# When VectorE turns the softmax denominators: small work moved between quarters of a unit, and the order of GpSimd's adds

## What is computed

```python
x = x + attention(layernorm(x), ctx, ctx)   # 32 query heads of 32 columns, 8 key/value heads,
                                            # softmax(q k^T / sqrt(32)) v
x = x + ffn(layernorm(x))                   # 8 small experts, the best one picked for each row
```

## Time and profile before

| | |
|---|---|
| median of three runs | 1024.35 us |
| the profiled execution | 1022.49 us |
| its span in the trace | 1020.7 us |
| granted TensorE clock, mean | 0.995 of full speed |

### The profile page before, as it was taken

The page is one execution under the profiler, slowest core; times in us unless marked ns, Lnnn a source line. Parts: engine busy times, 40 slices in busy tenths (PEclk is TensorE's granted clock), DMA queues, the critical chain, the costliest instruction groups (busy, mean ns, idle before and its releaser), DMA issues.

```text
span 1020.7 us, 24586 instructions
## 1 busy us (share of the span) xinstructions
PE 947.1 (93%) x9518; PEld 371.1 (36%) x9518; DVE 902.3 (88%) x1106; ACT 730.8 (72%) x1301; POOL 801.6 (79%) x454
## 2 busy tenths in 40 slices
PE   4789999999999999999999999999999999999996
PEld 3223333333333333333333323333222225777773
DVE  6979999999999999999999999998888886888976
ACT  5367788888888888888888877888777777554440
POOL 6259999999999999999999999999999998222110
PEclk9999999999999999999999999999999999999998
DMA  8674776767676767676867685756655744766423
GB/s 246 191 172 109 165 169 155 166 152 169 149 169 154 173 145 176 142 171 148 184 142 179 132 192 129 182 121 153 121 119 138 163 93 147 246 209 233 159 104 164
DMA packets 319875, 164.18 MB, mean 161 GB/s; under 512 B 182216, under 2 KB 307240, under 8 KB 319760
## 3 DMA queue, kind: packets, MB, share of 16 engines
q1 hardware_dynamic: 319456, 161.76, 64.3%
q0 software_dynamic: 304, 0.85, 0.4%
HBM read 107.58 MB, written 54.53 MB: 159 GB/s over the span
## 4 chain that ended last, share of the span: by engine, by line
PE 35%; DVE 31%; issue 25%; ACT 5%; POOL 3%; DMA 1%; SPq 0%; DVEq 0%; POOLq 0%; ACTq 0%
DVE row_max L927 14%; PE psum L590 8%; PE psum L604 6%; PE psum L617 5%; PE psum L735 5%; DVE den_t L939 4%; PE psum L552 4%; ACT probs L864 3%; PE psum L713 3%; DVE o_t L933 3%; DVE probs L1138 2%; PE psum L578 2%; DVE prod_mem L985 2%; PE psum L701 1%; ACT prod_mem L817 1%
## 5 line engine op out<-in xcount | busy, mean ns | idle before, releaser
L864 ACT ACTIVATE probs<-psum 128x512 f32<-128x512 f32 x1024 | 554.7, 596 | 131.0 <-PE psum L590 113.0
L927 DVE TENSOR_REDUCE row_max<-psum 128x4 f32<-128x2048 f32 x248 | 565.8, 2281 | 64.3 <-PE psum L552 64.0
L590 PE MATMUL psum<-q_stack,k_stack 97*32 97x512 f16 x4096 | 334.8, 386 | 9.9 <-issue 3.5
L365 POOL TENSOR_TENSOR sums<-probs 128x2048 f32<-128x2048 f32 x63 | 287.7, 4566 | 17.5 <-ACT probs L864 17.4
L353 POOL TENSOR_TENSOR sums<-probs 128x2048 f32<-128x2048 f32 x63 | 287.2, 4559 | 7.1 <-PE psum L627 5.5
L604 PE MATMUL psum<-probs,v_in 128*32 128x512 f32 x2048 | 268.8, 598 | 1.0
L590 PEld LDWEIGHTS psum<-q_stack,k_stack 97*32 97x32 f16 x4096 | 96.7, 95 | 258.8 <-ACT probs L864 149.2
L552 PE MATMUL psum<-high_mem 32*128 32x512 f16 x992 | 98.0, 384 | 23.7 <-DVE row_max L927 20.1
L325 POOL TENSOR_TENSOR o_t<-o_t,inv 128x512 f32<-128x512 f32 x64 | 67.2, 1049 | 40.7 <-DVE inv L945 38.8
L330 POOL TENSOR_TENSOR o_all<-o_all,o_t 128x512 f32<-128x512 f32 x64 | 81.6, 1274 | 9.2
L604 PEld LDWEIGHTS psum<-probs,v_in 128*32 128x32 f32 x2048 | 59.2, 110 | 60.9 <-issue 16.2
(11 more groups left out here) (119 smaller groups left out, 759.2 us busy)
## 6 DMA issues: line engine op xcount, KB each, us to landing
q_stack<-q_split SPq DMA_DIRECT2D x192, 128.0 KB, 3.4
xa<-in_x_dram SPq DMA_DIRECT2D x32, 512.0 KB, 4.7
o_all<-in_x_dram SPq DMA_DIRECT2D x256, 64.0 KB, 2.4
x_attended<-o_all SPq DMA_DIRECT2D x64, 256.0 KB, 4.1
out_dram<-probs SPq DMA_DIRECT2D x32, 512.0 KB, 2.9
q_split<-prod_mem SPq DMA_DIRECT2D x15, 1024.0 KB, 5.3
xa<-x_attended SPq DMA_DIRECT2D x16, 512.0 KB, 4.5
probs<-x_attended SPq DMA_DIRECT2D x16, 512.0 KB, 4.7
```

The costliest lines, as they stand in the source:

```text
L365: pool.tensor_tensor(sums[:, 2 * u % SUMS], probs[:, u % 2, 0], probs[:, u % 2, 1], ALU.add).then_inc(front_done, 1)
L590: last = pe.matmul(st_ps[row:row + D, bank_of["score", u, n], :], k_stack[:, u % SLOTS, t * P + row:t * P + row + D], q_stack[:, u % SLOTS ...
L864: act.activation(probs[:, s, keys, g, :], st_ps[:, bank_of["score", u, n], :], ACT.Exp, scale=EXP_SCALE).then_inc(exped, 1)
L927: dve.reduce_max(row_max[:, u % 2, t:G * ST:ST], s_ps[:], AX.X).then_inc(reduced, 1)
```

## The change

VectorE's list is changed in four places. The denominators of even units are turned in e1 instead of e0 (`DEN_AT`), behind that quarter's maxima, and their inverses are taken in e2 instead of e1. The inverses of odd units are taken in o3 instead of o1. The second half of a tile's moments moves from e1 to e2, and its variance from e2 to o1. In the planner, the denominator of an even unit is taken to keep its bank for 9 uses instead of 5. GpSimd adds the front pair of unit u ahead of the normalisation of unit u - 2 and of the inverse root, instead of behind them. No instruction is added or removed.

```diff
--- before.py
+++ after.py
@@ -195,7 +195,7 @@
 
             BEGIN = ((0, 4, 9, 13, NSC), (0, 4, 8, 12, NSC))
             MIDST = ((2, 6, 11, 15), (2, 6, 10, 14))
-            NORM_AT = 13
+            NORM_AT, DEN_AT = 13, 1
             DOWN_AT, FOLD_AT = ((-AHEAD, ST - 1), (1 - AHEAD, 0)), (1 - AHEAD, ST - 1)
 
             filled = [("part", n, i) for n in range(FIRST) for i in range(PIECES)]
@@ -211,7 +211,7 @@
                     filled += scores[half:]
                     if t == (ST - 1 if u % 2 == 1 else 2) and live(u - 1):
                         filled.append(("den", u - 1, 0))
-            KEPT = {"score": 2, "max": 2, "den": (5, 5), "part": 6}
+            KEPT = {"score": 2, "max": 2, "den": (9, 5), "part": 6}
             bank_of, bank_before, free_at, last_in = {}, {}, [0] * BANKS, [None] * BANKS
             for i, use in enumerate(filled):
                 bank = min(range(BANKS), key=lambda b: free_at[b])
@@ -355,15 +355,15 @@
                     if u == UNITS - 1:
                         for t in range(ST):
                             row_root(0, 0, t)
-                    if live(u - 2):
-                        normalise(u - 2)
-                    if u % 2 == 1 and whole(tile_of(u) + 1):
-                        inverse_root(tile_of(u) + 1)
                     if 0 <= u < UNITS - 1:
                         wait(pool, exped, NSC * u + NSC // 2)
                         wait(pool, den_done, u - 1)
                         pool.tensor_tensor(sums[:, 2 * u % SUMS], probs[:, u % 2, 0], probs[:, u % 2, 1],
                                            ALU.add).then_inc(front_done, 1)
+                    if live(u - 2):
+                        normalise(u - 2)
+                    if u % 2 == 1 and whole(tile_of(u) + 1):
+                        inverse_root(tile_of(u) + 1)
 
                 for n in range(ST + 2, TILES):
                     row_root(n // ST, n // ST % GROUPS, n % ST)
@@ -1032,19 +1032,19 @@
                             largest(*maxima_at(u, t))
                         if late and t < PIECES:
                             low_part(n, t)
-                        if t == 0 and live(u - 2) and u % 2 == 0:
-                            take_denominators(u - 2)
                         if u == UNITS and t == 0:
                             sum_last(1)
                         if t == 0 and live(u - 1):
                             take_rows(u - 1)
-                        if t == 1 and live(u - 2):
+                        if t == DEN_AT and live(u - 2) and u % 2 == 0:
+                            take_denominators(u - 2)
+                        if t == (DEN_AT + 1 if u % 2 == 0 else ST - 1) and live(u - 2):
                             invert(u - 2)
                         if early and t == 0 and u == 0:
                             first_moments(n + 1)
-                        if early and t == 1:
+                        if early and t == 2:
                             last_moments(n + 1)
-                        if early and t == 2:
+                        if late and live(u) and t == 1 and whole(n + 1):
                             variance(n + 1)
                             guard(n + 1)
                         if live(u) and u % 2 == 1 and t == ST - 1 and whole(tile_of(u + 1) + 1):
```

## The result

The changed kernel takes 1076.71 us in the median of four runs (1067.85 to 1077.35). The kernel before takes 1022.4 us, the median of the three runs above and a fourth of 1020.46 us. The ratio over all runs is 1.0513, with a 95% interval of 1.046 to 1.0566: slower by 5% (the medians alone give 1.053). The forecast was 1071 us, 1056 to 1081, slower with a chance of 0.88. The profiled execution is the 1067.85 us one, with a span of 1066.0 us; the other three took some 9 us more.

What follows compares the result with a forecast made beforehand. No engine was full; the handover between TensorE's score_rows and VectorE's maxima set the pair's length. Terms 24 x 1.6, 4 x 1.0, 2 x 0.66, 0.3 and 4.6 made 48.6 us; with 1022.5 that gave 1071 us, range 1056 to 1081.

Steps and rivals of the forecast that it cites:

- The bound and the maxima of e1: VectorE rules e0; with one transpose fewer there, the maxima of e1 start at 3.65 instead of 3.88, gaining 0.23 us a pair.
- The denominators: Turned behind the maxima of e1, they hold TensorE at tile 6 until 6.73 instead of 5.03; score_rows of e2 1.1 us late.
- What e2 adds: ScalarE's five late tiles delay the odd unit's denominators; score_rows of e3 comes at 11.3 instead of 9.69, 1.6 us late.
- The moves at no cost: Even and odd inverses, moments, variance and GpSimd's order fit into idle time or slack: cost 0.
- The tail: At u = 64 unit 62's transpose stands behind sum_last and take_rows, so project(0, 0) is late: 4.6 us, bounds 2 and 5.5.
- The sum: Over the whole kernel, the terms of the pairs and the end add 48.6 us to 1022.5, giving 1071 us.
- cheaper stall: Rival, chance 0.13: ScalarE catches up inside e2 and only 1.1 us a pair remain, so 1058 us.
- GpSimd ties in: Rival, chance 0.07: the 0.8 us slack at take_rows is gone, normalisation 0.5 late each pair, 15 us more: 1087.
- Faster: Rival, chance 0.07: TensorE reaches the tile later than 6.73, so den_taken costs no wait and the even spread pays: 1012 us.
- No change: Rival, chance 0.05: the bank is not as read and only the 0.23 us of e0 comes back: 1020 us.

Runs made afterwards that it cites:

- e0: Not a run: a quarter of the even unit in a pair of units; the kernel before turned the even denominators there.
- e3: Not a run: the quarter after e2 of the even unit in a pair; its score_rows was forecast at 11.3 instead of 9.69.
- The run with the wait at tile 4: The changed kernel with the planner's 5 uses of before, so the denominators' bank goes to tile 4 of e1: 1176.98 us, ratio 1.1501.

## Why the prediction was right

**The bound and the maxima of e1.** As forecast: the maxima of e1 start 3.64 us after `score_rows` of e0 (forecast 3.65), and e0 is TensorE's.

**The denominators.** The transpose starts at 5.85 (forecast 5.86), tile 6 at 6.61 (forecast 6.73), `score_rows` of e2 at 7.37 (forecast 7.39). TensorE goes on 0.05 us after the transpose's end, where I had taken 0.17 from the earlier trace rows.

**What e2 adds.** This term was too high by 0.2 us a pair. 0.12 us of it is the earlier tile 6. ScalarE starts its five tiles 0.45 us behind tile 6, and the odd unit's denominators come 3.0 us after that (430.81), where I had 3.1. They use the bank that ScalarE's small L796 frees behind the five tiles, at 430.71:

```profile
427.80 2.56 ACT L864 ACTIVATE probs<-psum 128x512 f32<-128x512 f32 x5 [1.85 <-PE psum L590]
430.44 0.27 ACT L796 ACTIVATE shift<-psum 16x128 f16<-16x128 f32 x1
```

`score_rows` of e3 comes at 11.07 instead of 11.3, which is 1.38 us late and not 1.6. Over 24 pairs I had 38.4 us and the profile shows 33.1. For tile 7 the pairs show 0.90 us (forecast 1.0), for tile 8 0.66 and 0.67 (forecast 0.66).

**The moves at no cost** are shown to be so by the run with the denominators put back. In detail the idle 0.57 us ahead of o3 took up the variance as said. GpSimd waits for the odd inverse in o3 as forecast:

```profile
447.16 1.05 POOL L325 TENSOR_TENSOR o_t<-o_t,inv 128x512 f32<-128x512 f32 x1 [1.30 <-DVE inv L945]
```

It ends that normalisation 2.2 us into the next pair (forecast 1.9), half a microsecond ahead of `take_rows`. The margin was thinner than I had it, and it held.

**The tail.** Forecast 4.6, measured 6.0. The first projection is 4.6 us late, as counted. The step left out that TensorE came out of this wait of 5.0 us at half its clock, which is the rest. `o_t` waited 3.99 us for GpSimd, and 4.00 before. GpSimd's long small instruction was not chance, for it came again beside `sum_last`:

```profile
891.38 2.29 DVE L1020 TENSOR_TENSOR sums<-probs 128x2048 f32<-128x2048 f32 x1 [2.72 <-PE psum L627]
```

```profile
892.01 1.80 POOL L343 TENSOR_SCALAR neg_mr<-mv,rstd 128x1 f32<-128x1 f32 x1
```

But it met the same L343 and not the small instruction before it, and GpSimd did not end where it had: counted from the last gather, `take_rows` started at 6.6 us instead of 7.1. That is the half microsecond which the term had counted back.

**The sum.** 33.1 + 4 x 0.9 + 2 x 0.66 = 38.0 us in the pairs before the last, with 6.0 in the tail and 1.5 for the one long pair, is 45.5; the two spans differ by 45.3. The forecast of 48.6 was too high for this execution. Its terms of e2 were 5.7 us too high, and the 1.4 us that the tail's term was too low and the 1.5 of the long pair took back a part. Against the medians, which differ by 54.3 us, it was too low, because the sum has no term for the clock: beside the tail's 1.4, six pairs at 1.53 us, 9 us in all, are in the profile of a typical run. Without both errors the sum would have met the median within 2 us. The two partly cancelled, which was luck: that the forecast lay 6 us under the median is not the whole size of the errors.

**The rivals.** What was seen lies between the forecast and *cheaper stall*: e2 does add to the 1.1 us, but 0.3 and not 0.5. *GpSimd ties in* did not happen: `o_t` waits for GpSimd once. *Faster* needed TensorE to reach the tile only when the bank was free; it was there early in each of the 31 pairs, by 1.27 us in the one shown. *No change* needed another bank than the planner gives; the bank was as read.

## What to carry to other kernels

When a reader of a shared buffer is moved later, look in the producer's own list for the first use of that buffer, and count all that stands behind it; the price is set there, not by the load of the reader's engine. A planner's number for how long a buffer is kept frees nothing: with the same late reader, 5, 9 and 14 uses gave 1177, 1077 and 1039 us. And where a quarter is ruled by one engine while it idles in the next, moving a piece of its own work over (one score tile, 0.8% faster) does what moving another engine's small work did not.

## What was not expected of the hardware

I had not expected the clock to answer to the change. In the kernel before all 632.76 us of the pairs with a tile ran at a granted clock of 1.00. With 1.27 us of idle in each pair, one pair of 31 in one execution and six in another ran into a stretch at half the clock (1.2 instead of 2.4 GHz), and cost 1.53 us more. The run with the denominators alone had six such pairs again, and the one with the tail put back five. With 3.02 us of idle every pair ran below 1.00, and the mean clock of the whole run fell to 0.918. Behind the 5.0 us of idle in the tail the clock was at half from 899 to 903 us, as the windows of the kernel after show (length, busy times, granted clock, DMA share, GB/s):

```profile
core 0: us, PE busy (x) PEld busy (x) DVE busy (x) ACT busy (x) POOL busy (x), PEclk, DMA share, GB/s
893.00:899.00 6.00, 1.08 (x10) 0.89 (x8) 1.99 (x3) 4.19 (x4) 4.15 (x6) 0.76 0.07 27
899.00:903.00 4.00, 3.92 (x17) 3.95 (x18) 1.60 (x4) 0.00 (x0) 3.24 (x5) 0.50 0.02 4
903.00:907.00 4.00, 4.00 (x37) 3.02 (x39) 0.44 (x1) 2.15 (x2) 0.13 (x1) 1.00 0.00 0
```

Between 893 and 899 TensorE worked 1.08 of 6 us. From 899 to 903 it was busy all the time, at 0.50, and from 903 at full speed again. Why equal pairs meet the fall in one execution and not in the other is open; no run here parts them.

The Trainium skill, "TensorE: Matmul & The Clock Gate", section "HAM oscillation — how this bites in real kernels", tells of a matmul loop that waits in each turn, and pays the fall of the clock in every turn instead of once. The run with the wait at tile 4 agrees: its pairs with a tile of `x` have a granted clock of 0.89 to 0.94, each one. The changed kernel, with 1.27 us of idle in a pair, paid in one turn of 31 or in six.
